# Normalising attention probabilities on GpSimd with two tensor products instead of four scalar products, in a two-layer transformer kernel

## What is computed

```python
x = x + attn0(cond(x, side, side, w0, u0, temb), ...)
x = x + ffn0(cond(x, side, side, w1, u1, temb), weight8)
x = x + attn1(cond(x, side, side, w2, u2, temb), ...)
x = x + moe(cond(x, side, side, w3, u3, temb), ...)

def cond(r, k, v, w, u, temb):      # two linear recurrences, forward and backward in time
    a = a * decay + exp(k) * v      # numerator, for each step
    b = b * decay + exp(k)          # denominator
    return sigmoid(r) * num / den * (0.8 + 0.2 * tf)

def attn(x):                        # 16 heads of 16, 256 queries, 256 keys
    scores = einsum('bhqd,bhkd->bhqk', q, k) / 4, causal mask
    att = softmax(scores, axis=-1)
    out = einsum('bhqk,bhkd->bhqd', att, v)
    return out @ Wo
```

## Time and profile before

| | |
|---|---|
| median of 3 runs | 735.11 us (733.54 to 739.29) |
| the profiled execution | 737.16 us, of which the span of the instructions is 735.3 us |
| mean granted clock of PE | 0.887 |
| busy: PE, DVE, POOL, ACT | 558.0, 463.3, 423.5, 329.3 us |
| first attention layer | about 41 to 216 us of the span |
| second attention layer | about 250 to 413 us |
| mixture of experts | from about 420 us to the end |

### The profile page before, as it was taken

The page is one execution under the profiler, slowest core; times in us unless marked ns, Lnnn a source line. Parts: engine busy times, 40 slices in busy tenths (PEclk is TensorE's granted clock), DMA queues, the critical chain, the costliest instruction groups (busy, mean ns, idle before and its releaser), DMA issues.

```text
span 735.3 us, 10992 instructions
## 1 busy us (share of the span) xinstructions
PE 558.0 (76%) x3284; PEld 413.2 (56%) x3284; DVE 463.3 (63%) x1051; ACT 329.3 (45%) x955; POOL 423.5 (58%) x445
## 2 busy tenths in 40 slices
PE   0348797888862797978888548925999999999960
PEld 0225455545531454545555334515999999999960
DVE  4736798797998377878978485203655555566510
ACT  4035474664763455646646612102444444444430
POOL 1106585674762165756757327770577777777772
PEclk9987998999955879989999958977999999999995
DMA  8999500000000000000000043326597778869623
GB/s 298 245 233 242 133 1 1 1 0 0 1 0 1 0 1 2 1 0 1 0 0 1 0 168 121 111 98 215 146 223 205 208 197 205 208 179 211 149 26 63
DMA packets 56706, 71.61 MB, mean 97 GB/s; under 512 B 11905, under 2 KB 45036, under 8 KB 56544
## 3 DMA queue, kind: packets, MB, share of 16 engines
q1 hardware_dynamic: 40272, 57.32, 27.6%
q0 software_dynamic: 16400, 13.87, 10.1%
HBM read 42.06 MB, written 37.04 MB: 108 GB/s over the span
## 4 chain that ended last, share of the span: by engine, by line
PE 53%; DVE 19%; ACT 9%; issue 8%; POOL 7%; DMA 2%; POOLq 0%; DVEq 0%; SPq 0%; ACTq 0%
PE S L860 13%; PE PJ L873 7%; PE PJ L612 6%; POOL xe_rows L382 5%; PE OB L699 5%; PE S L668 5%; DVE negmax L1045 4%; PE TB L683 4%; PE OB L873 4%; ACT prob L450 3%; DVE both L948 3%; DVE fwd L929 3%; PE TB L845 3%; PE PJ L654 3%; ACT probT L458 2%
## 5 line engine op out<-in xcount | busy, mean ns | idle before, releaser
L334 POOL TENSOR_SCALAR prob<-prob,rtotal 128x128 f32<-128x128 f32 (+1 forms) x256 | 173.4, 693 | 117.4 <-DVE rtotal L1051 95.2
L450 ACT ACTIVATE prob<-S,negmax 128x128 f32<-128x128 f32 (+1 forms) x256 | 104.0, 419 | 97.1 <-DVE negmax L1045 97.1
L860 PE MATMUL S<-xgT,wgu_s 128*128 128x384 f32 x576 | 109.6, 343 | 1.2 <-DVE hidden_f L1289 1.2
L1045 DVE TENSOR_REDUCE negmax<-S 128x2 f32<-128x256 f32 (+1 forms) x128 | 64.7, 546 | 71.2 <-PE S L671 71.0
L393 POOL DMA_INDIRECT out<-sig,y_token x48 | 75.5, 1573 | 47.7 <-ACT sig L586 35.3
L699 PE MATMUL OB<-probT,v_sb 128*32 128x256 f32 (+1 forms) x512 | 64.8, 382 | 48.2 <-ACT probT L458 48.2
L860 PEld LDWEIGHTS S<-xgT,wgu_s 128*128 128x128 f32 x576 | 100.3, 190 | 1.5 <-issue 1.4
L393 POOL DMA_INDIRECT odd_out<-sig,y_token x48 | 77.2, 1608 | 24.1 <-ACT sig L586 13.7
L668 PE MATMUL S<-k_sb,q_sb 32*128 32x128 f32 (+1 forms) x512 | 79.6, 388 | 7.5 <-ACT k_sb L475 7.5
L699 PEld LDWEIGHTS OB<-probT,v_sb 128*32 128x32 f32 x512 | 27.9, 121 | 78.8 <-ACT probT L458 33.0
L382 POOL DMA_INDIRECT xe_rows<-x_tok,slot_i x48 | 47.2, 984 | 38.5 <-ACT x_tok L551 24.1
(11 more groups left out here) (150 smaller groups left out, 952.2 us busy)
## 6 DMA issues: line engine op xcount, KB each, us to landing
xe_rows<-x8m SPq DMA_DIRECT2D x4, 3468.0 KB, 39.5
ratio<-xe_rows SPq DMA_DIRECT2D x32, 433.5 KB, 4.3
ratio<-in_wgu SPq DMA_DIRECT2D x32, 384.0 KB, 4.7
x8m<-in_wd SPq DMA_DIRECT2D x32, 256.0 KB, 2.9
x<-in_x SPq DMA_DIRECT2D x1, 1024.0 KB, 6.4
odd_out<-x8m SPq DMA_DIRECT2D x1, 1024.0 KB, 27.8
out<-side SPq DMA_DIRECT2D x8, 128.0 KB, 5.5
out<-odd_out POOLq DMA_DIRECT2D x1, 1024.0 KB, 7.8
```

Source lines behind the costliest of these rows:

```text
L334: ins = eng.tensor_scalar(p, p, rtotal[:, j % RING, st, h:h + 1], 1.0, ALU.mult, ALU.mult)
L450: ins = eng.activation(prob[:, j % RING, h, cols], S[:, 2 * (j % 2) + h, cols], ACT.Exp, bias=negmax[:, j % RING, st, h:h + 1], accum_out= ...
L860: ins = eng.matmul(S[:, m, 0:CAP], fast(wgu_s[:, j % 2, a, k, m * P:(m + 1) * P]), fast(xgT[:, j % 2, b, k, :]), start=n == 0, stop=n == N ...
L1045: ins = eng.tensor_reduce(negmax[:, j % RING, st, :], S[:, 2 * (j % 2):2 * (j % 2) + 2, cols], AX.X, ALU.max, negate=True)
```

## The change

```diff
                 eng.wait_ge(sem(f"rtotal_{L}"), v + 1)
                 settle(eng, "pool")
-                for h in range(2):
-                    for st, cols in HALVES:
-                        p = prob[:, j % RING, h, cols]
-                        ins = eng.tensor_scalar(p, p, rtotal[:, j % RING, st, h:h + 1], 1.0, ALU.mult, ALU.mult)
+                for st, cols in HALVES:
+                    p = prob[:, j % RING, :, cols]
+                    r = rtotal[:, j % RING, st, :].rearrange("p (h o) -> p h o", o=1)
+                    ins = eng.tensor_tensor(p, p, r.broadcast_to([P, 2, cols.stop - cols.start]), ALU.mult)
                 ins.then_inc(sem(f"normal_{L}"), 1)
```

## The result

The changed kernel takes 781.58 us (median of 4 runs, 779.27 to 783.49) against 737.20 us of the kernel before on the same chip: a ratio of 1.060 (95% interval 1.052 to 1.067), 44.4 us slower. A second measurement, beside the last experiments, gave 781.69 against 737.16 us, 1.062 (1.058 to 1.065). The profiled execution has a span of 781.6 us against 735.3, +46.3.

What follows compares the result with a forecast made beforehand. DVE, not POOL, was taken to bound the kernel. First pairs 0.8, holds net of DVE's waits 48.5 and PE's clock 4 gave +53 us: 790 profiled, 788 for the median of runs, range 762 to 828.

Steps and rivals of the forecast that it cites:

- the slack: DVE's waits in the other seven pairs of a batch: 1.3 us per batch absorbed, some 10 in eight batches.
- The sentence on two SBUF inputs: While POOL runs a sum or product of two tensors, a DVE instruction with two SBUF inputs stands still until it ends.
- The size of a hold: DVE instruction met by POOL's product: 0.9 us for 512 columns (0.6 for a pair of L936), 0.4 for 256.
- The first pair of each layer: Where PE has nothing else, undisturbed normalising costs 2.03 us instead of 1.66: 2 x 0.4 = +0.8 us.
- which instructions are met is fixed by DVE's order: After L1045 and L1051 POOL is released and DVE's condition work starts at once; holds per batch total 8.1 us.
- The list of pairs: Holds per batch: pairs 1, 3, 7 at 1.2 us each; 0, 2, 6 at 0.9; 4 at 0.8; 5 at 1.0.
- The sum per batch: Attention batch: 8.1 us of holds, less 1.3 of DVE's waits, plus 0.5 for PE's clock.
- The clock: With DVE later PE idles more and its clock falls; mostly hidden, 0.5 us per batch, +4 us.
- the bound: Upper limit for PE's lower clock: 5 us per batch, +40 us.
- rival 1: Lower PE clock in both attention layers, a slower result beyond the main case; chance 0.06.
- Rival 2: The spread second operand makes POOL's tensor product cheap; chance 0.10.
- Rival 3: Faster: two holds per pair instead of four release DVE sooner, 7 us gained, 728 us; chance 0.04.

Runs made afterwards that it cites:

- the same two waits: Kernel before, first L314 made to wait for L959's end and the second for query copy L1038: 734.51 against 737.16 us, ratio 0.995.

## Why the prediction was right, and where it wasn't

The forecast was 788 us with 762 to 828; measured 781.6. The direction, the engine and the mechanism held. The terms held less well: the holds were priced too high, a neighbour that moved was left out, and the slack was put too low. That these errors partly cancelled is why the total came within 7 us, and this closeness is luck.

**What bounds.** Right. DVE's share of the chain doubled, its busy time rose from 463.3 to 517.5 us where some 50 us more were forecast, its short waits vanished, and POOL's saved time bought nothing.

**A product of tensors holds DVE.** Right in kind: it needs no wait that the program wrote. L956, L966, L980 and the scans grew, L1045, L1051 and L1057 did not (two L1045 are 1.0 us before and after, L1051 is 0.17, two L1057 0.84). The run with four narrow tensor products and the one with two wide scalar ones show that the operation or the width alone does not make the cost: each alone has 11 and 12.5 us, 5 to 7 of them in the attention layers; together they have 44, and 36 to 37 in the layers. The sentence on two SBUF inputs was too narrow: its own row for L936 (1.20 us a pair against 0.61) is an instruction with one tensor input, and L959 (1.38 against 0.43), which was not on the list, is another.

**The size of a hold.** Too large. I priced 512 columns at 0.9 and 256 at 0.4 us per instruction met, and expected L966 at about 1.6 us; it is at 0.98. In the batch of rows 2 the wide one cost L956 0.57, L973 0.56, L980 0.47 and the second L929 0.75; the narrow one cost L948 and L966 0.24 and the first L929 0.42. The measured holds of the wide product lie 0.15 to 0.4 us below 0.9. One cause is the spread operand: the product takes 1.03 us instead of the 1.27 of L314. What makes up the rest isn't shown: DVE may hide part of a hold between two of its instructions, or POOL's instruction may not hold it for all of its length. The place was wrong in part, too: in pairs 2 and 6 the wide product was to meet the two L936 at 0.6 us; in the batch of rows 2 they keep their 0.34 us and the second scan L929 takes the 0.75.

**The first pair of each layer.** Forecast +0.8 us in all; measured none. Its piece of the chain in the second layer was 1.64 us and is

```profile
278.10 1.62 POOL prob L334 x2
```

again because the spread product is shorter than L314's rate gives: 0.60 + 1.03 us instead of the 2.03 forecast.

**What I didn't count: L314.** The step "which instructions are met is fixed by DVE's order" looked at DVE alone. The order within POOL stayed, but the shorter normalising put L314 0.6 us nearer, from beneath L1045 onto L959, at 0.9 us twice a batch; it also took it away from L929, where it had cost 0.5 us once. That is an estimate of 1.3 us a batch of DVE's time. In program time, net of what the same two waits give the kernel before, it is 13 us of the 44.5 by the medians and 3 to 4 by the layers. The list of pairs had 1.2 us for pairs 3 and 7 and 0.9 for pair 0. They became +1.4, +1.7 and -0.3.

**The sum per batch.** Forecast 8.1 less 1.3 of slack, plus 0.5 for the clock: 7.3. The batch of rows 2 grew by 5.8 us, the four middle batches by 5.1 on the mean. DVE's busy time in them grew by 7.3, of which some 1.3 are L314, so the normalising's holds made about 6.0 of the 8.1. The slack gave 2.2 instead of 1.3: the short waits went, and the long wait at the seam, which the forecast had left out of the slack, became shorter by some 0.4. A cost of the clock within a batch isn't to be seen: the second profile of the changed kernel has a granted clock of 0.79 in the second layer where the first has 0.85, and its middle batches are 0.2 us longer. From the first to the last maxima the forecast was 48.5 + 0.8 us, measured 38.2 and 39.4, of which 36.8 and 36.1 lie in the two layers and the rest between them. So the middle was 10 us too high.

**The clock.** Forecast +4, and +40 as the bound: no run shows either term, and both were the author's estimates. What is measured is a granted clock of 0.50 where the eight matmuls of the earlier trace rows take 1.50 us and of 1.00 where they take 0.84. Outside of the attention's maxima the changed kernel lost 8 and 5 us, of which 4.0 and 3.4 us in the windows above. That the number is near is luck. The forecast had it within the batches and from PE idling behind a later DVE. It lies behind the last batch, where versions with shorter batches have the low level as well; its cause is open. The bound of +40 was far off. The granted clock of the changed kernel is 0.86 and 0.82 in the first layer against 0.88, and 0.85 and 0.79 in the second against 0.89, so rival 1, the bound's clock in both layers, did not happen.

**The rivals.** Rival 2 (cheap spread operand) is true in part: the spread takes 0.22 us off the wide product and 12 us off the program (19 to 20 in the layers). That doesn't make it a scalar product: 512 columns take 1.03 us against 0.68, the latter from the run with two wide scalar products, with DVE at rest. Rival 3 (faster) is out: in the batch of rows 2 no pair but the one from which L314 went away became shorter.

## What to carry to other kernels

Before work on GpSimd is fused into fewer instructions, look at what VectorE does beside it: here an instruction of GpSimd that reads two tensors held up the VectorE instructions with two SBUF inputs that it met, and the wide scaling ones too (0.24 to 0.95 us each). The same 768 columns cost 11 us in four pieces and 44 in two, and a per-partition scalar is worth keeping as a scalar. Weigh small costs together and not one by one: VectorE's waits hid about 2 us per batch, once. When a new version of one kernel gains by moving a neighbour, try the same move in the old one before the gain is booked. When an instruction gets shorter, follow what is queued behind it to where it lands now; where that matters, tie it by a semaphore to a moment when the other engine reads from PSUM or waits (here that took L959 from 1.38 us back to 0.43).

## What was not expected of the hardware

- On GpSimd a product with a spread second operand is faster than with one of full width: 1.03 against 1.25 us for 512 columns, 0.60 against 0.72 for 256. The slope is 1.67 against 2.09 ns a column; the scalar product has 0.83.
- A hold cost the held instruction less than the holder's length: 0.24 to 0.42 us with a 256-column product of 0.60 us, 0.47 to 0.75 with one of 1.03 us.
- A VectorE operation with a single tensor input, L959 (`tensor_scalar`, 128 x 512, f32, SBUF to SBUF), is held like one with two: 1.38 us beside L314 against 0.43 with GpSimd at rest.
- An instruction of GpSimd that only writes held VectorE too: beside a clearing of 0.52 us the scaling L936 took 0.95 us instead of 0.34, in five places.
- The stretch behind the last attention pair took 14.0 us at a granted clock of 1.00 and 18.0 at 0.50 or 0.52, and kernels that differ only in the place of L314 lie on both sides; why is open.
